# Fusing the key/value projection with the attention over 8192 context rows, with scores taken in four row groups of 32

## The reference

```
x = x + cross_attention(layernorm(x), ctx)     # 16 heads of 32, keys and values projected from ctx
x = x + self_attention(layernorm(x))           # over a sequence of length one: only Wv and Wo matter
x = x + ffn(layernorm(x))                      # 8 experts, the best 2 of each row, gelu, 512 -> 2048 -> 512

cross_attention: q = x Wq + bq; k = ctx Wk + bk; v = ctx Wv + bv
                 softmax(q k^T / sqrt(32)) v, then Wo and bo
```

## Time and profile before

| | us |
|---|---|
| median of 3 runs (lowest to highest) | 1449.85 (1448.89 to 1450.54) |
| the profiled execution, its own time | 1445.7 |
| its span, first to last instruction | 1443.9 |
| key/value projection, from 29.9 to 388.5 in the span | 358.6 |
| attention, from 396.4 to 987.4 | 591.0 |
| PE / DVE / ACT / POOL busy | 1370.8 / 950.6 / 772.9 / 73.6 |

### The profile page before, as it was taken

The page is one execution under the profiler, slowest core; times in us unless marked ns, Lnnn a source line. Parts: engine busy times, 40 slices in busy tenths (PEclk is TensorE's granted clock), DMA queues, the critical chain, the costliest instruction groups (busy, mean ns, idle before and its releaser), DMA issues. The chain is left out here.

```text
span 1443.9 us, 20528 instructions
## 1 busy us (share of the span) xinstructions
PE 1370.8 (95%) x7608; PEld 847.3 (59%) x7608; DVE 950.6 (66%) x819; ACT 772.9 (54%) x841; POOL 73.6 (5%) x71
## 2 busy tenths in 40 slices
PE   5999999999799999999999999998769999999995
PEld 4888888888643333333333333333557787887873
DVE  7444444444288888888888888887653566766662
ACT  4122221221088888888888888884222445555541
POOL 2000000000030000000000000000102010111110
PEclk9999999999999999999999999999955999999998
DMA  6854555556396555555555555520804666676641
GB/s 207 266 175 179 193 199 184 174 193 196 136 260 131 112 112 112 112 109 114 116 116 116 116 116 116 114 61 1 306 5 147 220 216 211 232 243 206 239 132 40
DMA packets 140900, 225.07 MB, mean 156 GB/s; under 512 B 8776, under 2 KB 41672, under 8 KB 140848
## 3 DMA queue, kind: packets, MB, share of 16 engines
q1 hardware_dynamic: 137520, 217.12, 51.7%
q0 software_dynamic: 3344, 7.47, 2.1%
HBM read 162.61 MB, written 59.85 MB: 154 GB/s over the span
## 5 line engine op out<-in xcount | busy, mean ns | idle before, releaser
L663 ACT ACTIVATE at_p<-at_s 128x1024 f32<-128x1024 f32 x512 | 496.9, 1023 | 90.7 <-PE at_s L616 90.6
L683 DVE TENSOR_TENSOR p_sum<-p_sum,at_p 128x2048 f32 (+1 forms) x208 | 476.7, 2292 | 58.1 <-ACT at_p L663 51.1
L616 PEld LDWEIGHTS at_s<-q_stack,at_k 97*128 97x128 f32 x1024 | 172.7, 189 | 248.5 <-ACT at_p L663 162.0
L616 PE MATMUL at_s<-q_stack,at_k 97*128 (+1 forms) x1024 | 311.4, 424 | 7.5 <-PEq L444 6.7
L629 PE MATMUL at_o<-at_p,at_v 128*32 128x512 f32 x2048 | 272.7, 605 | 0.1
L143 ACT ACTIVATE sc_c_hi<-sc_c 128x2048 fp32r<-128x2048 f32 x16 | 30.7, 1920 | 151.0 <-PE sc_vp L388 137.6
L413 ACT ACTIVATE sc_k_hi<-sc_kp,sc_bk 128x512 fp32r<-128x512 f32 x64 | 44.2, 691 | 125.4 <-PE sc_kp L381 125.4
L345 DVE SCALAR_TENSOR_TENSOR sc_k_lo<-sc_kp,sc_bk,sc_k_hi 128x512 fp32r<-128x512 f32 x64 | 47.8, 749 | 89.0 <-ACT sc_k_hi L413 89.0
L353 DVE TENSOR_TENSOR sc_v<-sc_vp,sc_bv 128x512 f32<-128x512 f32 x64 | 44.1, 689 | 88.8 <-PE sc_vp L388 88.8
L1268 ACT ACTIVATE se_h<-se_hp,se_b_cur 128x160 f32<-128x160 f32 x128 | 43.4, 391 | 105.4 <-PE se_hp L1203 105.4
L1255 ACT ACTIVATE se_wi_hi<-ei_wi 128x2048 fp32r<-128x2048 f32 x32 | 61.2, 1913 | 69.4 <-DVE se_b_cur L1314 69.1
(11 more groups left out here) (225 smaller groups left out, 1534.4 us busy)
## 6 DMA issues: line engine op xcount, KB each, us to landing
at_k<-k_hi_scratch SPq DMA_DIRECT2D x128, 256.0 KB, 4.8
ei_wi<-w_in SPq DMA_DIRECT2D x32, 1024.0 KB, 7.4
ei_wo<-w_out SPq DMA_DIRECT2D x32, 1024.0 KB, 5.5
sc_c<-ctx_t SPq DMA_DIRECT2D x16, 1024.0 KB, 7.9
k_hi_scratch<-sc_k_hi SPq DMA_DIRECT2D x16, 1024.0 KB, 4.0
k_lo_scratch<-sc_k_lo SPq DMA_DIRECT2D x16, 1024.0 KB, 6.1
at_k<-k_lo_scratch SPq DMA_DIRECT2D x64, 256.0 KB, 4.2
at_v<-v_scratch SPq DMA_DIRECT2D x64, 256.0 KB, 4.9
```

Source lines behind the costliest of these rows:

```text
L616: last = nc.tensor.matmul(s[r][:, a * NQ:(a + 1) * NQ], k[c][:, j, t * P:(t + 1) * P], q_stack[:, bass.ds(it // PER_GROUP * (HG * NQ) + j ...
L663: nc.scalar.activation(p[t % PR][:, pair * 2 * NQ:(pair + 1) * 2 * NQ], s[u % SR][:, :], ACT.Exp, scale=SCALE).then_inc(p_ready[t % PR], 1)
L683: nc.vector.tensor_tensor(sums, sums, p[t % PR][:, :], ALU.add).then_inc(p_summed[t % PR], 1)
```

## The change

`stream_context`, `find_maxima`, `load_keys` and `attend` are replaced by one block, `attend_stream`. Keys and values no longer go through DRAM and there is no `q_stack`: scores are made from `q_hi`, `q_lo`, `k_hi`, `k_lo` where they lie. A step is one key tile of 128 rows with one group of four heads; a chunk has 16 steps (four groups by four tiles), 256 steps in all, taken two by two ("doubles"). While a chunk's steps run, the next chunk is projected.

PE, per double j of chunk n (the first double of all has no projection and no outputs; the last chunk projects nothing after its first double):

```diff
+            def scores(i, b, step):
+                n, g, t = 2 * i + b, step // KT, step % KT
+                if t == 0:
+                    pe.wait_ge(k_lo_ready, NG * n + g + 1)
...
+                for pair in range(2):
+                    u = (b * STEPS + step) * 2 + pair
+                    if u >= SR:
+                        w = u - SR
+                        pe.wait_ge(p_ready[w // 2 % PR], exped(2 * i, w // 2, w % 2))
...
+                for part, (keys, queries) in enumerate(((k_hi, q_hi), (k_lo, q_hi), (k_hi, q_lo))):
+                    for j in range(HG):
+                        rows, r = slice(j * D, (j + 1) * D), ((b * STEPS + step) * 2 + j // 2) % SR
+                        last = nc.tensor.matmul(s[r][:, j % 2 * NQ:(j % 2 + 1) * NQ], keys[rows, g, t * P:(t + 1) * P],
+                                                queries[rows, g, :], start=(part == 0), stop=(part == 2))
+                        if part == 2 and j % 2 == 1:
+                            last.then_inc(s_ready[r], 1)
+            def outputs(n, b, step):
+                g, t = step // KT, step % KT
+                if t == 0:
+                    wait_reuse(pe, o_added, NG * n + g)
...      # four fp32 products with a 128x32 weight, as at L629
+                    for j in range(DOUBLES):
+                        for half in range(2):
+                            scores(i, b, 2 * j + half)
+                            if j == 0 and not begins:
+                                project(n, b, *OUTPUTS[-1], proj[:, :], False, half)
+                            elif j > 0 and not ends:
+                                project(n + 1, 1 - b, *OUTPUTS[j - 1], proj[:, :], False, half)
+                        for step in (2 * j - 2, 2 * j - 1):
+                            if step >= 0:
+                                outputs(n, b, step)
+                            elif not begins:
+                                outputs(n - 1, 1 - b, step + STEPS)
```

`project` makes one output (12 products, six in each half) in the one bank `proj`; `OUTPUTS` is v0, k0, v1, k1, v2, k2, v3, k3, so an odd double ends a value output and an even one a key output. The first chunk is projected ahead of the loop, into eight banks. ACT and DVE:

```diff
+                    for j in range(DOUBLES):                       # ACT
+                        exps(i, b, 2 * j, (0, 1))
+                        if 2 <= j < 2 + ET and not last:
+                            split(n + 2, b, j - 2)
+                        exps(i, b, 2 * j + 1, (0,))
...      # keep: copies proj to v, or to k_hi with its bias
+                        exps(i, b, 2 * j + 1, (1,))
+                    for j in range(DOUBLES):                       # DVE
+                        add_probabilities(n, 2 * j)
...      # keep_low in the even doubles: k_lo from proj and k_hi
+                        if j % 2 == 1 and j > 1:
+                            add_outputs(n, (j - 3) // 2)
+                        elif j == 1 and not begins:
+                            add_outputs(n - 1, NG - 1)
+                        if 2 <= j < 2 + ET and not last:
+                            split(n + 2, b, j - 2)
+                        add_probabilities(n, 2 * j + 1)
```

The general paths go to one block at the end, `any_path`, which holds the whole layer again in eight stages, each skipped by a branch of its own on one flag:

```diff
+    def guarded(self, eng, name):
+        if name not in self.flags:
+            self.flags[name] = eng.value_load(self.flag[:, :], min_val=0, max_val=1)
+        with eng.If(self.flags[name] > 0):
...
+            self.programs[name](eng)
```

More of the change, by code:

```diff
@@ L309, in pair @@
[L309 to L316, removed]
@@ L319, in _ @@
[L319 to L327, removed]
@@ L328, in _ @@
[L328 to L336, removed]
+                    begins, ends = isinstance(n, int) and n == 0, last and b == 1
+                    for j in range(DOUBLES):
[10 more added lines that the diff above has]
+                                outputs(n - 1, 1 - b, step + STEPS)
@@ L340, in pair @@
                     n = 2 * i + b
[L341 to L347, removed]
@@ new lines, in _, with cross_output @@
+            dve.wait_ge(a.biases, 16 * (1 + NG))
+            for (kind, i), bank in zip(OUTPUTS, first_banks):
+                if kind == "k":
+                    keep_low(0, i, bank)
+            for d in range(ET):
+                split(1, 1, d)
+            rolled(dve, PAIRS, pair)
+            add_outputs(NCH - 1, NG - 1)
+def cross_output(nc, ctx, opened, u, wo, bo, bv, o_acc, p_sum, x_sb, good):
+    sb = lambda n, s, d=F32: ctx.enter_context(nc.sbuf_tensor(u + n, s, d))
+    sem = lambda n: ctx.enter_context(nc.semaphore(u + n))
@@ L730, in _ @@
                 last.then_inc(totalled, 1)
+            pe.wait_ge(widened, NG + 1)
+            for g in range(NG):
+                last = nc.tensor.matmul(out[0][:, :], bv_wide[:, g, :], wo[:, g, :], start=(g == 0), stop=(g == NG - 1))
+            last.then_inc(bias_done, 1)
+            pe.wait_ge(bias_added, 1)
             for g in range(NG):
@@ L1357, in _, with __init__, next, __enter__ @@
             keep_tail(NX - 1)
-def run_experts(nc, ctx, rounds, w_in, b_in, w_out, ident, x_sb, out_dram, r, inputs):
-    u = f"ex{rounds[0]}_"
+class General:
+    def __init__(self, nc, block, flag, met):
+        self.nc, self.block, self.flag, self.met = nc, block, flag, met
+        self.stage, self.flags = 0, {}
+    def next(self):
+        self.stage += 1
+        self.programs = {}
+        self.retired = list(self.nc.released_uncleared_semaphores)
+        return lambda: self
+    def __enter__(self):
+        return self
+    def sync(self, program):
+        self.programs["sync"] = program
+    def gpsimd(self, program):
+        self.programs["gpsimd"] = program
+    def vector(self, program):
+        self.programs["vector"] = program
+    def tensor(self, program):
+        self.programs["tensor"] = program
+    def scalar(self, program):
+        self.programs["scalar"] = program
+    def guarded(self, eng, name):
+        if name not in self.flags:
+            self.flags[name] = eng.value_load(self.flag[:, :], min_val=0, max_val=1)
+        with eng.If(self.flags[name] > 0):
+            if name == "gpsimd":
+                for first in (n for n in self.retired if n - 1 not in self.retired):
+                    end = next(n for n in range(first, first + len(self.retired) + 1) if n not in self.retired)
+                    self.nc.gpsimd.sem_clear(range(first, end))
+            self.meet(eng, 2 * self.stage - 1)
+            if name in self.programs:
+                self.programs[name](eng)
+            self.meet(eng, 2 * self.stage)
+    def meet(self, eng, times):
+        eng.drain()
+        eng.sem_inc(self.met, 1)
+        eng.wait_ge(self.met, 5 * times)
+    def __exit__(self, *failure):
+        if failure[0]:
+            return
+        @self.block.sync
+        def _(sp):
+            self.guarded(sp, "sync")
+        @self.block.gpsimd
+        def _(pool):
+            self.guarded(pool, "gpsimd")
+        @self.block.vector
+        def _(dve):
+            self.guarded(dve, "vector")
+        @self.block.tensor
+        def _(pe):
+            self.guarded(pe, "tensor")
+        @self.block.scalar
+        def _(act):
+            self.guarded(act, "scalar")
@@ L1400, in run_experts @@
         "sel_ready", "sel_turned", "sel_t_ready", "gathered", "xg_ready", "scattered", "x_stands"))
-    def guarded(eng, program):
-        flag = eng.value_load(r.long[:, :], min_val=0, max_val=1)
-        with eng.If(flag > 0):
-            program()
-    with nc.Block() as block:
+    with opened() as block:
         @block.sync
@@ L1503, in scatter, with output_biases @@
                 last.then_inc(scattered, 1)
+            def output_biases():
+                for t in range(QT):
+                    last = nc.tensor.matmul(bias_banks[t], r.combine_t[:, t * P:(t + 1) * P], r.bo[:, :],
+                                            start=True, stop=True)
+                last.then_inc(biased, 1)
             def expert(e, last):
@@ new lines, in perceiver_layer @@
+        a.c_loaded = [sem("as_c_loaded")]
+        weights = whole.enter_context(ExitStack())
+        a.w_hi, a.w_lo = (weights.enter_context(nc.sbuf_tensor(f"as_w_{n}", [P, ET, 2 * E], F32R, side="right")) for n in ("hi", "lo"))
+        late, at = [], nc.sbuf_top
+        for n, shape in (("xwo", [P, ET, E]), ("xbo", [P, E]), ("swv", [P, ET, E]), ("sbv", [P, ET]), ("swo", [P, ET, E]), ("sbo", [P, E])):
+            late.append(nc.alloc_sbuf_tensor_at(n, shape, F32, offset=at))
+            at += max(4 * math.prod(shape[1:]), 32)
```

1221 lines of the change are left out of this document (688 added, 533 removed).

## The result

The changed kernel takes **1526.01 us** (median of 4 runs, 1523.62 to 1528.35), the kernel before 1449.37 beside it (1448.73 to 1450.54): ratio 1.0528, 95% interval 1.0509 to 1.0547. It is 5.3% slower; I forecast 1436 us, 1% faster. The time lies inside my whole range, 1395 to 1560, but that is luck: above 1465 the range was there for loads in file, and that isn't what happened. The span of the profiled execution is 1523.3 us, 93.6 more than the 1429.7 of my sum. (The time is some 90 over the forecast, as the profiled execution lay 4.15 under the median before and 0.95 under it here.)

A forecast was written before the change was run, and what follows sets the result against it. PE was taken to bound both replaced stages. The block saves 17.7 us and the rest adds 3.5, so the profiled span goes from 1443.9 to 1429.7; forecast 1436 us (chance 0.67), own range 1408 to 1465, whole range 1395 to 1560.

The forecast's parts named there:

- loads in file: Rival in the block's scores: weight loads of four row groups follow one another, 1.35 us a step; 1552 us, chance 0.22.
- Less score work: Block's scores on PE: twelve products on 32 rows, four side by side, cost 0.70 us a step.
- Changes of tile shape: PE in each double: five changes, three between 32 and 128 rows at 0.06 us, the others 0.20 and 0.11.
- The wait for `o_added`: Odd doubles: PE idles 1.5 us ahead of its outputs, since DVE adds behind the first probability sum; double 7.93 us.
- The sum of the block: Start, 60 odd and 60 even doubles, last seven and drain: ends at 970.3 us against 988.0, 17.7 less.
- Start and last chunk: Block's start: first exponentials done at 58.6 us; last seven doubles, without projection, 46.2 us.
- The end: Kernel's end: eight branches instead of one, 1.0 us for each of seven more, +7 us (0 to 15).
- The rest of the kernel: Outside block and end: `turn_tokens` -2.5 us by fewer shape changes, `cross_output` -1 us (bounds -4 and +4).
- the rivals: Loads in file (1552 us, chance 0.22), row groups not side by side (1857, 0.03), no wait for `o` (1334, 0.08).

The follow-up runs named there:

- run 10: Changed kernel with finished outputs added ahead of the double's first probability sum and each projected output made in one piece of twelve products: 1422.41 us.
- Run 1: Changed kernel with DVE adding the finished group of outputs ahead of the double's first probability sum instead of behind it: 1441.8 us.
- Runs 2 to 4: Changed kernel with the block's loop written out on PE, ACT and DVE: 1490.15 us; on PE only: 1481.11; two pairs of chunks per PE loop body: 1499.37.
- run 3: Changed kernel with only PE's loop of the attention block written out in eight copies, ACT and DVE keeping their loop: 1481.11 us.
- run 7: Changed kernel with the eight stages of the unused general path behind one branch on each engine instead of eight: 1497.03 us.
- Runs 7 and 8: Changed kernel with one branch on each engine around the eight unused stages: 1497.03 us; with the unused general path removed altogether: 1493.39 us.

## Why the prediction was wrong, by its steps

**Less score work: right.** Four row groups run side by side: bursts 0.23 us apart, a step's scores 0.70 and 0.2 of changes. "Loads in file" is refuted by the four weight loads of a burst that end 0.19 after its start. The Trainium skill ("TensorE: Matmul & The Clock Gate", Part 3) has the rule that loads of different row groups overlap; the trace agrees.

**Changes of tile shape: mis-sized.** I took 0.06 for a change between 32 rows and 128 from the earlier trace rows, with 0.20 as the bound. Measured is the bound: 705.14 - 704.25 - 0.70 = 0.19, 706.73 - 705.14 - 1.40 = 0.19, and 0.195 by run 10. The double is 6.83, forecast 6.45, bound 6.87. From the earlier trace rows I took off 0.11 for the other's weight load, as if it were no part of the change; in the block the load is not ahead of its product after a change, so it may be part of the cost. The rule that I weighed and set aside, that a change of mode drains the engine (the Trainium skill, "TensorEngine Tiling (Array Packing)", Key Properties), is nearer to the trace than what I took: a product of another shape starts 0.33 after the last one, of some 0.40, and its weight load isn't ahead of it; a full drain in the profile's modelled times it isn't. How much is drain and how much load no run separates. Yet only the even doubles paid: 16.4 us in all, since in odd ones the wait shrank by as much as PE grew.

**The wait for `o_added`: right, place, order and the double's length.** Forecast an odd double of 7.93, measured 14.69 - 6.83 = 7.86. PE's idle part of it is 1.0 us on average (61.6 in 59) and not 1.5, since PE arrives later by its dearer changes of shape. But I booked it as a fixed part of the change. Run 1 shows it as its largest flaw, four lines and 84 us.

**The sum of the block: a term was missing.** I took the loop for free, as the loops before are. The five pairs with a jump back are 7.4 us longer each than the regular ones, 36.9 of the 38.4: some 5 us idle and the rest by the 1.2 GHz behind it. Runs 2 to 4 show that it is the jump: 35.9 us come back with the loop written out. No row of the kernel before could show it, but the diff did show that one turn of PE's loop grows from some 430 instructions to 1780, a resource that the trace had never tried. It should have stood as an unknown with an upper end.

**Start and last chunk: the clock.** 12 us in the last chunk: I forecast 12.75 for a pair without projection; measured are 15.3, 14.6 and 18.2, as PE waits 2.8 us for `o_added` in each odd double and then goes on at 0.50. With the wait gone they are 10.25 to 10.6. From its first addition to the last one starting it takes 54.9 us here, 49.9 in run 3's trace and 51.4 in run 7's, with nearly the same waits and a higher clock (0.83 and 0.81 against 0.73), so its length isn't fixed by the code. Of the 7.2 at the start, 1.9 is PE's later first product (31.85, before 29.9), 1.6 its half pace over the first eight, 1.28 a table load ahead of the exponentials, the only one in the block; the other 2.4 I put down to the clock, which is 0.50 from 61.3 to 67.3, behind 4.4 us of waiting for the exponentials.

**The end: the bound was wrong.** I gave 1.0 us for each further branch with 2.1 as the upper end, from SP's wait in the earlier trace rows. Runs 7 and 8 show 3.3 to 3.5. The better row was one I had: the earlier trace rows, where reading a flag and skipping an unused block takes 6.1 us in the middle of the kernel, with a meeting of the engines in it; it allows more than 2.1. A compare-and-branch is some 108 ns by the Trainium skill ("Advanced Engine Details and Errata", Control Flow Timing). Neither the skipped stages nor the long jumps back here cost so little.

**The rest of the kernel: no error seen**, -2.1 against -3.5. The traces can't tell these apart: the same code takes 442.0 to 448.5 us in the traces of the other runs.

Shape changes, jumps, last chunk, start and end together are 92.3 of the 93.6. None of the rivals was it: PE's path was as short as the forecast had it but for the changes of shape, and what came on top were idle stretches and the slow clock behind them. The rival on the slower side, loads in file, had the sign right and its mechanism wrong.

## What to carry to other kernels

In a fused block, ask of every wait on the bound engine what is queued ahead of the releasing instruction on its own engine, and put the releaser first; look for this before counting products. Count the instructions in a loop's turn, not only the work: past some length each jump back can cost microseconds, and so can every stage that is skipped by a branch of its own. An idle stretch costs more than its length where PE then runs at its lower clock: 7.4 us for some 5 here. Where buffers are taken in turn inside a loop, see that a turn's uses divide by their number, or that the wait at its head is early enough.

## What the runs showed of the hardware that I had not expected

- A jump back over some 1780 or 3550 PE instructions leaves PE idle for 4.7 to 5.5 us in this block, with 430 or 860 in the old loop nothing, with 3020 there 1.84 us.
- A change between 32-row and 128-row weights costs PE 0.19 to 0.20 us, as much as one from 128 columns to 32; back from the outputs to scores it is 0.10 (709.21 to 711.07, less 1.76).
- Each stage skipped at the end behind a branch of its own takes 3.3 to 3.5 us, one branch around all eight 4.7. Whether a short stage costs as much no run shows.
